# Feeding the shared expert's second half from stored halves in place of transposing h2 again, and a new order of the transposes in the opening

## The reference, cut to what matters

```python
x = L0_attn_x                                    # (1, 2048, 512)
mod = (silu(c) @ wmod) -> sa, ca, ga, sb, cb, gb # six rows of 512; ga, gb kept 0.25 away from 0
h = layernorm(x) * (1 + ca) + sa
x = x + ga * (tanh(h @ B.T) @ C.T + D * h)       # 256 states
h = layernorm(x) * (1 + cb) + sb                 # "h2" in the kernel
scores = sigmoid(h @ gate_w.T)                   # 8 experts, the best 2 of scores + router_bias
routed = sum over the 2 experts of w * (silu(h @ W1) * (h @ W3)) @ W2       # 352 hidden
shared = (silu(h @ sw1.T) * (h @ sw3.T)) @ sw2.T                            # 704 hidden
x = x + gb * (routed + shared)
```

## Time and profile before

| | before |
|---|---|
| median of three runs | 567.3 us (567.28 to 568.34) |
| the profiled execution | 568.31 us, its span 566.6 us |
| PE busy | 545.8 us, 96% |
| DVE busy | 301.5 us, 53% |
| POOL busy | 263.2 us, 46% |
| ACT busy | 181.1 us, 32% |
| transposes of h2 and of the tiles of `step` (L929) | 272 on PE |
| bytes moved | 107.19 MB, mean 189 GB/s |

### The profile page before, as it was taken

One profiled execution on the slowest core, in us unless ns is written; L12 is line 12 of the kernel. 1 busy time (PEld: TensorE's weight loads), 2 busy tenths in 40 slices (PEclk: granted clock), 3 DMA queues, 4 the chain that ended last, 5 costly groups with the idle time before them and its releaser, 6 DMA issues.

```text
span 566.6 us, 11166 instructions
## 1 busy us (share of the span) xinstructions
PE 545.8 (96%) x3184; PEld 490.3 (87%) x3185; DVE 301.5 (53%) x631; ACT 181.1 (32%) x347; POOL 263.2 (46%) x221
## 2 busy tenths in 40 slices
PE   8997799999999999999999999999999999999995
PEld 3666688988999999899999999999999999889994
DVE  3788776696677667632222222222222222479886
ACT  1444346345443442133222322232222322222210
POOL 2599886677667456443053430053535100245531
PEclk9998999999999999999999999999999999999998
DMA  8999245331332597566255754267676222367744
GB/s 306 395 330 333 75 153 219 131 111 74 111 122 103 175 331 292 185 225 223 95 185 203 278 183 178 90 215 267 214 259 206 91 74 74 112 208 221 225 157 137
DMA packets 41113, 107.19 MB, mean 189 GB/s; under 512 B 4224, under 2 KB 4224, under 8 KB 41088
## 3 DMA queue, kind: packets, MB, share of 16 engines
q1 hardware_dynamic: 28288, 54.44, 27.3%
q0 software_dynamic: 12800, 52.43, 26.8%
HBM read 76.19 MB, written 30.67 MB: 189 GB/s over the span
## 4 chain that ended last, share of the span: by engine, by line
PE 82%; POOL 6%; DVE 5%; issue 3%; DMA 2%; ACT 1%; SPq 0%; DVEq 0%; POOLq 0%
PE bank L946 15%; PE bank L947 14%; PE bank L948 14%; PE bank L962 8%; PE bank L960 8%; PE bank L961 8%; PE bank L929 5%; PE bank L967 4%; PE bank L898 2%; PE bank L900 2%; PE bank L899 2%; DMA x_all<-wmod 2%; POOL x_all L552 1%; POOL tmpa L544 1%; POOL tmpa L549 1%
## 5 line engine op out<-in xcount | busy, mean ns | idle before, releaser
L946 PE MATMUL bank<-whi,thi 128*128 (+1 forms) x416 | 139.0, 334 | 0.0
L947 PE MATMUL bank<-wlo,thi 128*128 (+1 forms) x416 | 134.6, 324 | 0.0
L948 PE MATMUL bank<-whi,tlo 128*128 (+1 forms) x416 | 134.3, 323 | 0.0
L536 POOL TENSOR_TENSOR wlo<-raw,whi 128x1408 f32 (+3 forms) x24 | 79.7, 3334 | 87.2 <-DMA whi<-w_all 75.0
L960 PE MATMUL bank<-whi,gth 128*128 (+1 forms) x204 | 80.9, 396 | 2.4 <-DVE gtl L1668 1.3
L962 PE MATMUL bank<-whi,gtl 128*128 (+1 forms) x204 | 80.6, 395 | 0.0
L961 PE MATMUL bank<-wlo,gth 128*128 (+1 forms) x204 | 79.9, 391 | 0.0
L1653 DVE TENSOR_TENSOR gbuf<-s,bank 128x352 f32<-128x352 f32 x52 | 27.1, 521 | 98.5 <-ACT s L873 97.6
L947 PEld LDWEIGHTS bank<-wlo,thi 128*128 128x128 f32 x416 | 78.5, 189 | 0.0
L946 PEld LDWEIGHTS bank<-whi,thi 128*128 128x128 f32 x416 | 78.5, 189 | 0.0
L948 PEld LDWEIGHTS bank<-whi,tlo 128*128 128x128 f32 x416 | 78.3, 188 | 0.0
(11 more groups left out here) (201 smaller groups left out, 970.3 us busy)
## 6 DMA issues: line engine op xcount, KB each, us to landing
raw<-w_all POOLq DMA_DIRECT2D x8, 2176.0 KB, 10.4
whi<-w_all POOLq DMA_DIRECT2D x16, 704.0 KB, 11.5
h<-xs_rows SPq DMA_DIRECT2D x36, 256.0 KB, 2.7
ys_rows<-tmpa SPq DMA_DIRECT2D x36, 256.0 KB, 2.0
x_all<-wmod SPq DMA_DIRECT2D x6, 1024.0 KB, 9.9
whi<-w_all POOLq DMA_DIRECT2D x8, 768.0 KB, 4.6
hs_rows<-h SPq DMA_DIRECT2D x8, 512.0 KB, 2.9
h<-hs_rows SPq DMA_DIRECT2D x16, 256.0 KB, 2.7
```

What stands on the lines that cost most here:

```text
L536: pool.tensor_tensor(wlo[:, bass.ds(off + (SH + a), b - a)], raw[:, a:b], whi[:, bass.ds(off + (SH + a), b - a)].bitcast(F32), ALU.subtrac ...
L946: pe.matmul(dst, xh[:, j, a], wh, start=(m == 0), stop=False)
L947: pe.matmul(dst, xh[:, j, a], wl, start=False, stop=False)
L948: mm = pe.matmul(dst, xl[:, j, a], wh, start=False, stop=(m == KD - 1))
```

## The change

- Two new DRAM tensors, `xt_high` and `xt_low`, 4 MB each. In section A SP stores `xah` and `xal` of each pair there (`store_x`, two DMAs of 512 KB), between `rows_of_pair` and the store of h2. ACT waits for that store (`s_xts`) before it writes `xah` for the next pair.
- The 16 tiles of sections B and C are no longer loaded to `xin` and transposed. SP loads their high and low parts straight to `xbh` and `xbl` (`load_x`, two DMAs of 256 KB for a tile), as soon as the `up` product two tiles before has ended. PE's `up` waits for them. Their 64 transposes, 16 copies on ACT and 16 subtractions on DVE go away. The routed tiles keep theirs.
- The transposes of S0 stay at the start of step B3; the last step of S, now written out of its loop, has none.
- The loads of S0 and S1 no longer wait for a transpose, but for all stores of `xah` and `xal`.
- In the opening, PE's iteration it = 3 does the transposes of h2 of pair 0 and the attention of pair 1 ahead of `turn_t` of pair 2, which now writes banks 6 and 7 in place of 2 and 3. ACT and DVE take the high and low parts in the same order. The copy of the gate weights on ACT moves ahead of `states(1, 2)`.

```diff
             def body(it, lo, hi):
                 if lo == NP + 2:
+                    sp.wait_ge(s_stp, NP)
+                    sp.wait_ge(s_xts, 32 * (NP - 1))
+                    for t in range(2):
+                        load_x(t, t)
                     sp.wait_ge(s_nat, NP * 16)
-                    sp.wait_ge(s_h2T, NP)
-                    for t in range(2):
-                        load(hs, t, t * P)
                     sp.wait_ge(s_xd, NP)
                     rows_of_pair(NP - 2, 1)
                     sp.wait_ge(s_scat, 64 * (NP - 2))
...
+                if live(3, lo, hi):
+                    store_x(it - 3)
                 if live(2, lo, hi):
                     p = it - 2
                     sp.wait_ge(s_h2, p * 2 + 2)
...
+            def load_x(t, j):
+                for dst, src in ((xbh, xth), (xbl, xtl)):
+                    sp.dma_start(dst[:, j, :].bitcast(F32), src[t * P:(t + 1) * P, :]).then_inc(q["C", "xin"][j], 16)
+
+            def store_x(p):
+                sp.wait_ge(q["A", "xlo"], p * 2 + 2)
+                for dst, src in ((xth, xah), (xtl, xal)):
+                    sp.dma_start(dst[bass.ds(p * 2 * P, 2 * P), :].rearrange("(b p) d -> p b d", p=P),
+                                 src[:, :, :].bitcast(F32)).then_inc(s_xts, 16)
...
-            def next_c(s, j, tile):
-                sp.wait_ge(q["S", "xt"], s * 2 + (j + 2 + NB))
-                load(hs, 1 - j, tile * P)
+            def next_c(k):
+                if k < NT - NB:
+                    sp.wait_ge(q["S", "up"], iters * 2 + (NB + k - 1))
+                    load_x(NB + k, k % 2)
...
             for t in range(2, NB):
-                sp.wait_ge(q["S", "xt"], t - 1)
-                load(hs, t % 2, t * P)
+                sp.wait_ge(q["S", "up"], t - 1)
+                load_x(t, t % 2)
+            sp.wait_ge(s_xts, 32 * NP)
+            sp.wait_ge(s_h2T, NP)
             sp.wait_ge(s_pad, 48)
...
             for n in range(3):
                 row = row_of(n)
-                sp.wait_ge(q["S", "xt"], NB - 1 + n)
+                if n > 1:
+                    sp.wait_ge(q["S", "xt"], n - 1)
                 load(xs, n % 2, row)
...
             def high_a(p, lo):
                 act.wait_ge(s_h2T, p + 1)
                 if lo > 3:
                     act.wait_ge(q["A", "up"], p * 2)
+                    act.wait_ge(s_xts, p * 32)
...
                 if lo == NP + 2 and j == 1:
-                    high(0, 0, bank[6])
                     scores(NP - 1)
...
+                if loaded is not None:
+                    pe.wait_ge(q["C", "xin"][j], loaded * 32)
+                elif sec == "A":
+                    pe.wait_ge(q["A", "xlo"], i * 2 + (j + 1))
...
             def body(it, lo, hi):
-                if live(1, lo, hi):
+                if live(1, lo, hi) and lo != 3:
                     turn_t(it - 1, lo)
...
                 if live(2, lo, hi):
                     attention(it - 2, lo)
-
+                if lo == 3:
+                    turn_t(it - 1, lo)
...
                 if lo == NP + 2:
                     ranks(it - 4)
-                    turn(0, 0, bank[6])
...
+        def routed_next(i, j, c, sec):
+
+            if sec == "B":
+                return i * 2 + j == NB - 1
+            return sec == "S" and not (c == -1 and j == 1)
...
+                if routed_next(i, j, c, sec):
+                    pe.wait_ge(q["A", "y"], NT)
+                    if sec == "S" and not (isinstance(i, int) and i + j == CB):
+                        pe.wait_ge(q["S", "xlo"], (i - CB) * 2 + j)
                     turn(i + j, 1 - j, bank[j])
```

More of the change, by code:

```diff
@@ L322, in steps @@
                     step(i, j, None, "S")
-            with eng.Fori(CB + 2, iters + CB) as i:
+            with eng.Fori(CB + 2, iters + (CB - 1)) as i:
                 for j in range(2):
                     step(i, j, None, "S")
+            for j in range(2):
+                step(iters + (CB - 1), j, -1, "S")
             first = NP - 1 if unrolled else CB + 2
@@ L468, in _ @@
             store_y(iters - 3, 1)
[L469 to L472, removed]
+            store_y(iters - 2, 0)
+            for j in range(2):
+                next_c(j)
+                store_y(iters + (j - 2), 1 - j)
             for c in range(CB, NP):
                 for j in range(2):
-                    if 2 * c + j + 3 < NT:
-                        next_c(iters + (c - CB), j, 2 * c + j + 3)
-                    if c + j == CB:
+                    k = (c - CB) * 2 + j
+                    next_c(k + 2)
+                    if k == 0:
                         store_y(iters - 1, 1)
-                    elif 2 * c + j + 3 < NT:
+                    elif k < NT - NB - 3:
                         store_out(c - 1 + j, 1 - j)
@@ L840, in _ @@
             modulation(4)
+            act.wait_ge(l_gate, 32)
+            act.activation(whi_a[:, :, 0:E], gw[:, :, :], ACT.Copy).then_inc(s_gwh, 1)
             states(1, 2)
@@ L858, in step @@
                 first, last = sec == "B" and i + j == 0, sec == "C" and isinstance(c, int) and c * 2 + j == NT - 1
[L859 to L863, removed]
+                if routed_next(i, j, c, sec):
+                    act.wait_ge(q["S", "up"], i * 2 + j)
                     high(i + j, 1 - j, bank[j])
-                if not last and not early:
-                    next_high()
                 act.wait_ge(q["S", "up"], i * 2 + (j + 1))
@@ L980, in turn_t @@
                     pe.wait_ge(s_lg, (p - 3) * 2 + 2)
+                if lo == 3:
+                    pe.wait_ge(s_tanh, p * 2)
+                    pe.wait_ge(s_sign, 2)
+                    pe.wait_ge(s_abs, 2)
                 for j in range(2):
-                    mm = transposes(bank[2 + j], tbuf[:, j, :])
+                    mm = transposes(t_bank(lo, j), tbuf[:, j, :])
                 mm.then_inc(s_tT, 1)
@@ L1046, in body @@
                         pe.wait_ge(s_gwl, 1)
-                    if live(1, lo, hi):
+                    if live(1, lo, hi) and lo > 3:
                         pe.wait_ge(s_tlo, (it - 1) * 2 + 2)
@@ L1132, in step @@
                         before = pe.snap(off_b[1 - j], min_val=0, max_val=WSZ)
-                def next_turn():
-                    if first:
-                        pe.wait_ge(q["A", "y"], NT - 1)
-                    else:
-                        pe.wait_ge(q["A", "y"], NT)
-                        pe.wait_ge(q["S", "xlo"], i * 2 + j)
+                if routed_next(i, j, c, sec):
+                    pe.wait_ge(q["A", "y"], NT)
+                    if sec == "S" and not (isinstance(i, int) and i + j == CB):
+                        pe.wait_ge(q["S", "xlo"], (i - CB) * 2 + j)
                     turn(i + j, 1 - j, bank[j])
-                if not last and not early:
-                    next_turn()
                 if first:
@@ L1415, in between @@
                         route(it - 4, lo, *which)
-                if live(1, lo, hi) and lo > 1:
+                if live(1, lo, hi) and lo > 1 and lo != 3:
                     turned_low(it - 1, lo)
@@ L1420, in body @@
                     lows_a(it - 3, lo)
+                if lo == 3:
+                    turned_low(it - 1, lo)
                 if lo == 2:
@@ L1499, in body @@
                 if lo == NP + 2:
-                    lows(0, 0, bank[6])
                     between(*range(KM + 1, KR))
@@ L1629, in step @@
                 first, last = sec == "B" and i + j == 0, sec == "C" and c * 2 + j == NT - 1
-                early = sec == "B" and i == 0
-                def next_lows():
-                    if not first:
-                        dve.wait_ge(q["S", "up"], i * 2 + j)
+                if routed_next(i, j, c, sec):
+                    dve.wait_ge(q["S", "up"], i * 2 + j)
                     lows(i + j, 1 - j, bank[j])
-                if not last and not early:
-                    next_lows()
                 if sec == "B" and i * 2 + j == 1:
```

47 lines of the change are left out of this document (23 added, 24 removed).

## The result

The changed kernel takes 571.91 us (median of 5 runs, 571.03 to 573.01) against 567.54 us for the kernel before on the same chip (5 runs, 567.28 to 568.70): a ratio of 1.0067, 95% interval 1.0053 to 1.0080. It is slower by 4.4 us. The forecast was 567.1 us, and its range 563.6 to 569.6.

The account below looks back on a forecast made before the run. PE, 96% busy, was taken as the bound, except for POOL's chain in the opening and DMA waits at S0 and C's gathers; 0 + 0 + 3.2 - 3.4 = -0.2 us from 567.3 gave 567.1 us, range 563.6 to 569.6.

Parts of the forecast that it names:

- section C's gain: PE time saved on tiles 4 to 15, -3.4 us, forecast to be given back ahead of S0.
- two halves of the same delay: Waits at B2 and S0, behind pair 7's store in SP's queue, counted once within the 3.2 us.
- the 1.57 MB: Extra bytes in SP's queue ahead of S0, competing with the last eight scatters; 4.2 us later at 373 GB/s if shared.
- The share: How SP's and POOL's queues divide the engines before S0: full sharing 4.2 us, giving way 0; 3.2 us taken.
- The scatters: Last scatters before S0 land later, delaying the first routed load: +3.2 us; rival of no delay, 563.9 us, chance 0.35.
- The clock: Rival: PE's clock halves after idling ahead of S0, losing 1.7 us, for 568.8 us; chance 0.27.
- Tiles 4 to 15: Section C: twelve sets of transposes at 0.40 us saved, less losses to gathers and loads: -3.4 us (-3.8 to -2.5).
- what the gathered rows keep: C0 to C5: the late gather holds DVE, so 1.0 us of the 2.0 us saved there is lost.
- the 0.4 for bytes: Section C: charge for 512 KB loads a step beside the gathers, 0.4 us, bounds 0 and 1.3.
- Section A: ACT's wait for the pair's store before writing xah, up to 1.4 us late for pair 7: 0, bound 0.5.
- The opening: Reordering in the opening gains 0 (bounds -0.4 and +0.2); PE's idle time reappears in front of turn_g.

Follow-up runs that it names:

- e1: Changed kernel with the last pair's halves stored after the first routed loads instead of ahead of the loads of tiles 2 and 3: 567.64 us, ratio 0.9987.
- e2: Changed kernel with pair 7's store between the loads of tile 3 and the first routed loads: 573.38 us, ratio 1.0076.
- e10: Changed kernel with pair 7's store between tile 3's loads and the routed loads, SP not waiting for it until before C's loads: median 571.0 us, 1.0072.
- e8: Changed kernel with low-half loads of tiles 4 to 15 cut to 16 of 128 partitions: 570.89 us, ratio 1.0048.
- e6: Changed kernel with the store of a pair's halves ahead of the routing's rows in iterations up to 9: 571.01 us, ratio 1.0061.
- the combined kernel: Changed kernel, last store behind first routed loads, finish_first one step later in C, earlier stores ahead of routing's rows: 563.91 us (0.9921), again 562.41 us (0.9904).

## Why the prediction was wrong, by its own steps

**Where the gain was given back: right in kind, wrong in place.** The forecast said that the loads and the store in SP's queue would eat section C's gain ahead of S0. They did, but before B2, and up to S1 for twice the price (6.15 us against 3.2).

**The step that failed** is the sentence that PE "may wait first at B2 and then at S0; they are two halves of the same delay and are counted once". B2's wait was never priced. It needed a sum of its own: the bytes in SP's queue ahead of tile 2's load, divided by SP's share. The prediction divided the 1.57 MB by the 373 GB/s of all engines and asked what that does to the scatters; tile 2's load does not see 373 GB/s but 109. The runs with the store elsewhere show it: behind the routed loads (e1) B2's wait is gone, and between the loads (e2, e10) too.

That the idle time agrees, 4.8 us forecast (1.6 + 3.2) and 4.92 measured, is luck: it is another wait, with another sum. Taking it as divided between B2 and S0 is also what spoke against the loss by the clock.

**The share.** The rows of the two queues were read as not telling how they share. They held what mattered: 936 packets of q0 are 3.60 MB, 3.85 KB each, and 206 of q1 0.36 MB, 1.75 KB each. The text said that both queues move rows of 2 KB; q0 also carries the weights. In the changed kernel, with both queues full for most of the time, 1462 and 1201 packets go out side by side, 55 to 45, while the bytes divide 72 to 28. An estimate with equal numbers of packets, from the rows of before: SP's part of 373 GB/s is 1.75 / (1.75 + 3.85) = 31%, 117 GB/s; 2.1 MB take 18.0 us from 201.85 on and, with 2.6 us of latency, have landed at 222.5. In the change PE ran dry at 218.99, and the trace of before has it at tile 2's products at 219.55, 0.4 us of transposes included: a wait of 3.3 to 3.5 us could have been forecast. The Trainium skill ("DMA: Bandwidth & Descriptors", section on queues, rings and completion order) has the engines alternate between queues by packets. The trace's 55 to 45 is near that, if what it counts as a packet, 4.0 and 1.9 KB here, stands for the page's; no run here tests it.

**The scatters: +3.2 forecast, 2.7 measured, and worth nothing.** The routed load is issued at 225.88 in place of 223.22, but PE is later still. With the store away it is 224.41 (e1), so by difference 1.5 us are the store's and about 1.2 the loads' of tiles 2 and 3. There PE does wait for it, 1.48 us, as the prediction had it for the whole.

**The clock: the rival was right in its mechanism.** It stood at S0 with 1.7 us and a chance of 0.27. It came at B2, after 4.92 us of idle time, a little longer than the 4.3 us from which it was said to decide, and cost 2.5 us. This is the largest thing that the sum left out.

The sum for this step: 4.9 idle, 2.5 of clock, less 0.4 for the transposes that are gone, 7.0; measured 14.01 - 7.20 = 6.8.

**Tiles 4 to 15: -3.4 forecast, -2.4 measured** (S1's +6.15 to C11's +3.71). The price of 0.40 us for four transposes holds to the hundredth: steps are 6.30 us. Mis-sized was what the gathered rows keep. C0 to C5 was to shorten by 1.0 less the 0.4 for bytes; it became 0.4 us longer. The 0.4 us for a slower gather was too small, and its bound of 1.3 us too: the gather needed 2.0 us more. That the bytes are the reason is not shown (e8). Nor was the excess of 2.3 us before due to this gather alone: most of it stood in the step to C3, and there it shrank, from 1.95 to 1.29.

**Section A: 0 forecast with a bound of 0.5.** ACT's wait was 2.20 us, PE's 0.9, in iteration 9. With it gone (e6) S1 comes 0.8 us earlier, so the term was 0.8 us, above its bound.

**The opening: 0 forecast, 0 measured**, by itself (0.9992) and in the change. PE's idle time went in front of other instructions, as POOL's chain demands. It stands not in front of `turn_g` alone but in front of three instructions.

With the parts as measured (-0.2 at B1, +6.8 in the step to B2, -0.4 from there to S1, -2.4 from S1 to C11) the sum is +3.8 us, as is the difference of the spans. Beside the forecast's -0.2 that is 3.9 us too much: 2.5 by the clock, 1.0 in C, and 0.4 that lie within what section A cost.

## What to carry to other kernels

When a transfer is added to a queue, price every later transfer of that queue by the queue's own share of the engines, for which packets and bytes side by side gave a good estimate here, and not by what all engines move; the first one that an engine waits for is the bound, and it may stand well ahead of the one that you had in mind. A saving per step lasts only until the next wait whose end does not move with it: list what stands in each engine's order ahead of the critical instruction (here `finish_first` ahead of `gtl`) and take it out of that place first. The same change became 5 us faster than the kernel before by order alone: a store behind the loads that are waited for, DVE's work on gathered rows one step later, and the other stores ahead of a long read.

## What the runs showed of the hardware

A wait of 4.9 us on PE cost another 2.5 us by the clock, which stood at 0.50, the 1.2 GHz level, for some 6 us, whereas six products of zeros in the same gap, 5.3 us of work, kept it at 1.00. In four profiles of this family (the change, the combined kernel, and the runs with the lighter loads and with the store between) ACT stood still for 2.1 to 3.5 us in C3 with its input ready, the releaser named remote; in the other runs with the same ACT program it did not. In the change it ends with DVE's wait for the gather, within 0.2 us; in the combined kernel, where DVE has no such wait, the step took 2.3 us more. What it waits for is not settled: in the change and in the combined kernel the queue of instructions moves no packet in those microseconds.
